# Third feed-forward stage of a Flamingo-style block stack: experts on masked inputs, accumulated in PSUM, instead of experts on all inputs, selected on VectorE

## The reference

```python
def _L2_ffn_ref(x, Wg, bg, We, be):
    ...
    probs = jax.nn.softmax(x @ Wg + bg, axis=-1)
    idx = jnp.argmax(probs, axis=-1)
    p = jnp.take_along_axis(probs, idx[..., None], axis=-1)[..., 0]
    e_idx = idx % We.shape[0]
    h = jax.nn.relu(jnp.einsum('bsd,edf->besf', x, We) + be[None, :, None, :])
    onehot = jax.nn.one_hot(e_idx, We.shape[0], dtype=x.dtype)
    out = jnp.einsum('besf,bse->bsf', h, onehot) * p[..., None]
    return out
...
    x = x + jnp.tanh(g_ffn[2]) * _L2_ffn_ref(_layernorm(x, axis=-1), L2_ffn_Wg, L2_ffn_bg, L2_ffn_We, L2_ffn_be)
```

## Time and profile before

| | |
|---|---|
| median of 3 runs | 1844.87 us |
| lowest and highest | 1843.51 and 1848.87 us |
| span of the profiled execution | 1861.1 us |
| own time of the profiled execution | not among the runs' times; its span stands 16.2 us over their median |
| mean granted clock of TensorE, whole span | 0.886 |
| stage F2, from the last addition to x of A2 to its own last one | 779.03 to 939.78 us, 160.75 us |
| PE, DVE, ACT busy, whole span | 75%, 72%, 55% |

### The profile page before, as it was taken

One profiled execution on the slowest core, in us unless ns is written; L12 is line 12 of the kernel. 1 busy time (PEld: TensorE's weight loads), 2 busy tenths in 40 slices (PEclk: granted clock), 3 DMA queues, 4 the chain that ended last, 5 costly groups with the idle time before them and its releaser, 6 DMA issues.

```text
span 1861.1 us, 35910 instructions
## 1 busy us (share of the span) xinstructions
PE 1404.8 (75%) x9844; PEld 1054.7 (57%) x9844; DVE 1333.1 (72%) x4156; ACT 1024.2 (55%) x2876; POOL 492.1 (26%) x499
## 2 busy tenths in 40 slices
PE   3677776987734446676769998989997409999995
PEld 3455554665523334433325666666666408999995
DVE  3888886888879986889945667766766455666665
ACT  3677785432425553311037777767785326777773
POOL 5433530221100001100000032232233333555451
PEclk9999998999965557978789999999999758999998
DMA  7000069300199910000000000000000052222226
GB/s 167 7 7 6 12 83 160 48 0 1 34 145 157 162 18 17 28 1 0 1 6 1 7 26 22 16 29 23 10 23 24 27 223 61 64 66 68 64 64 227
DMA packets 144711, 97.75 MB, mean 53 GB/s; under 512 B 21658, under 2 KB 133934, under 8 KB 143443
## 3 DMA queue, kind: packets, MB, share of 16 engines
q1 hardware_dynamic: 135890, 79.49, 23.2%
q0 software_dynamic: 8704, 16.87, 2.8%
HBM read 42.43 MB, written 54.93 MB: 52 GB/s over the span
## 4 chain that ended last, share of the span: by engine, by line
PE 36%; issue 31%; DVE 17%; ACT 9%; POOL 2%; DMA 1%; SPq 1%; another core or an unknown queue 1%; DVEq 1%; ACTq 0%; POOLq 0%
PE bank L1227 6%; PE bank L1219 6%; PE bank L863 5%; PE bank L912 3%; PE bank L879 3%; ACT att L1383 2%; ACT arena L1260 2%; PE bank L899 2%; PE bank L889 2%; DVE nm L1699 2%; PE bank L867 2%; DVE att L1700 1%; DVE tmp L1977 1%; DVE arena L1843 1%
## 5 line engine op out<-in xcount | busy, mean ns | idle before, releaser
L1260 ACT ACTIVATE arena<-bank 128x512 f32<-128x512 f32 (+6 forms) x440 | 255.5, 614 | 141.2 <-PE bank L1083 61.5
L540 POOL TENSOR_TENSOR rstd<-ve,mhalf 128x4 f32<-128x4 f32 x64 | 67.0, 1046 | 688.2 <-DVE ve L1680 688.2
L1383 ACT ACTIVATE att<-bank,arena 128x128 f32<-128x128 f32 x512 | 181.5, 377 | 81.8 <-DVE arena L1843 79.9
L1615 ACT ACTIVATE att<-bank,arena 128x128 f32<-128x128 f32 x576 | 164.6, 371 | 69.9 <-PE bank L1219 67.6
L639 POOL DMA_INDIRECT dispatched_rows<-arena x128 | 132.5, 1035 | 222.0 <-DVE arena L1761 153.5
L690 POOL DMA_INDIRECT expert_outputs<-arena x144 | 144.7, 1005 | 148.1 <-issue 102.9
L1260 ACT ACTIVATE xnT<-bank 128x128 f32<-128x128 f32 (+1 forms) x180 | 63.4, 352 | 190.2 <-PE bank L711 134.8
L1227 PE MATMUL bank<-arena,att 128*128 128x128 f32 x1152 | 154.1, 277 | 3.0 <-ACT att L1615 1.9
L1219 PE MATMUL bank<-xnT,arena 128*128 128x128 f32 x1152 | 154.1, 277 | 0.2 <-ACT xnT L1260 0.2
L1227 PEld LDWEIGHTS bank<-arena,att 128*128 128x128 f32 x1152 | 141.0, 193 | 5.3 <-ACT att L1615 5.3
L1219 PEld LDWEIGHTS bank<-xnT,arena 128*128 128x128 f32 x1152 | 141.6, 194 | 0.8 <-ACT xnT L1260 0.8
(11 more groups left out here) (324 smaller groups left out, 3306.1 us busy)
## 6 DMA issues: line engine op xcount, KB each, us to landing
dispatched_rows<-padf SPq DMA_DIRECT2D x16, 2128.5 KB, 35.4
arena<-dispatched_rows SPq DMA_DIRECT2D x144, 64.5 KB
cxT<-in_ctx SPq DMA_DIRECT2D x32, 256.0 KB, 2.7
arena<-in_L_ffn_w SPq DMA_DIRECT2D x8, 1024.0 KB
arena<-expert_outputs SPq DMA_DIRECT2D x8, 1024.0 KB, 13.7
expert_outputs<-arena POOLq DMA_INDIRECT x144
dispatched_rows<-arena POOLq DMA_INDIRECT x128
out_x<-x SPq DMA_DIRECT2D x8, 256.0 KB, 4.8
```

Source lines behind the costliest of these rows:

```text
L1260: copy = lambda o, i: nc.scalar.activation(o, i, ACT.Copy)
L1383: last = nc.scalar.activation(ex3_of(w, side)[:, i, :], bank[side][:, i * P:i * P + P], ACT.Exp, bias=nm3[:, w % 2, h:h + 1], accum_out=su ...
L1615: last = nc.scalar.activation(h3[:, s % 2, k * P:k * P + P], bank[s % 2][:, k * P:k * P + P], ACT.Gelu, bias=b1c3[:, s % 4, k:k + 1])
```

## The change

Each tile's normalised rows are multiplied by their one-hot column, once for each expert: eight copies of the tile, of which each row is non-zero in one alone (`xm2`). The tiles 0 and 2 of a chunk are masked by one DVE operation of 128 x 1024 each, the tiles 1 and 3 by eight ACT operations of 128 x 128 each. PE transposes the eight copies (`masked_T`, two banks), ACT copies them out of PSUM (`xmT2`), and PE multiplies each by its expert and adds all eight products, after a product of the one-hot rows with the biases, in one PSUM group (`experts`). The ReLU is ACT's (`activated`), the addition to x stays on DVE (`residual2`), one chunk late. The biases of gate and experts are split in three bf16 parts in the set-up of the stage on POOL (`parts`) and go into PSUM by small products; the exponentials take the greatest value as their bias and sum as they go. `xm2` and `xmT2` have two slots, by the tile's parity. Elsewhere the diff only lets several waits share one semaphore (`s_setup`, `F3_routing`, `F0_gate_up`), and loads bg in 3 rows and be three times.

```diff
@@ tiles @@
-        oh2 = [ar([P, CB, E2]) for _ in range(2)]
-        ohT2 = ar([E2, W])
-        acc2 = ar([P, CB, P])
+        oh2 = [ar([P, CB, 3 * E2]) for _ in range(2)]
+        ohT2 = [ar([3 * E2, W], BF16) for _ in range(2)]
+        xm2, xmT2 = ar([P, 2, E2, P]), ar([P, 2, E2, P])
+        relu2 = ar([P, CB, P])
@@ gpsimd, before the powers of F2 @@
+            def parts(whole, rest, part, mask):
+
+                for i in range(3):
+                    step(pl.tensor_copy(part[i][:, :], whole[:, :]))
+                    if i < 2:
+                        step(pl.tensor_tensor(rest[:, :], whole[:, :], part[i][:, :], ALU.subtract))
+                    whole = rest
+                for i in range(3):
+                    step(pl.tensor_scalar(part[i][:, :], part[i][:, :], mask(i), None, ALU.mult))
+                step(pl.tensor_tensor(part[0][:, :], part[0][:, :], part[1][:, :], ALU.add))
+                pl.tensor_tensor(part[0][:, :], part[0][:, :], part[2][:, :], ALU.add).then_inc(sem("F2_constants"), 1)
...
+            parts(be2, berest2, bepart2, lambda i: bemask2[:, i:i + 1])
+            parts(bg2, bgrest2, bgpart2, lambda i: ident[0:3, i:i + 1])
@@ tensor @@
+            def masked_T(c, j):
+
+                pe.wait_ge(sem("F2_masked_even" if j % 2 == 0 else "F2_masked_odd"), c * 2 + (j // 2 + 1))
+                pe.wait_ge(sem("F2_mT"), c * CB + (j + 1))
+                for e in range(E2):
+                    last = nc.tensor.transpose(bank[2 + j % 2 * 2 + e // 4][:, e % 4 * P:e % 4 * P + P], xm2[:, j % 2, e, :], ident[:, :])
+                last.then_inc(sem("F2_mT_full"), 1)
+
+            def experts(c, p, j):
+
+                pe.wait_ge(sem("F2_mT"), c * CB + (j + 3))
+                if j == 0:
+                    pe.wait_ge(sem("F2_ohT"), c + 2)
+                    pe.wait_ge(sem("F2_relu"), c + 1)
+                y = bank[6 + p][:, j * P:j * P + P]
+                nc.tensor.matmul(y, ohT2[p][:, j * P:j * P + P], bepart2[0][:, :], start=True, stop=False)
+                for e in range(E2):
+                    last = nc.tensor.matmul(y, xmT2[:, j % 2, e, :], we2[:, e * P:e * P + P], start=False, stop=(e == E2 - 1))
+                last.then_inc(sem("F2_y"), 1)
+
+            def f2(c, p, more):
+
+                for j in range(CB):
+                    if j == 0 and more:
+                        chunk_T(c + 1, 1 - p)
+                    if j == 1 and more:
+                        logits(c + 1)
+                    if j < CB - 1:
+                        masked_T(c, j + 1)
+                    experts(c, p, j)
+                if more:
+                    chosen(c + 1, 1 - p)
+                    masked_T(c + 1, 0)
@@ scalar @@
+            def exponentials(c):
+                act.wait_ge(sem("F2_onehot"), c + 1)
+                for j in range(CB):
+                    last = nc.scalar.activation(ex2[:, j, :], bank[1][:, j * P:j * P + P], ACT.Exp, bias=nmx2[:, j:j + 1], accum_out=ps2[:, j:j + 1])
+                last.then_inc(sem("F2_exp"), 1)
+
+            def masked(c, p, j):
+                act.wait_ge(sem("F2_onehot"), c + 1)
+                act.wait_ge(sem("F2_mT_full"), c * CB + (j + 1))
+                for e in range(E2):
+                    last = nc.scalar.activation(xm2[:, 1, e, :], xn2[p][:, j, :], ACT.Copy, scale=oh2[p][:, j, e:e + 1])
+                last.then_inc(sem("F2_masked_odd"), 1)
+
+            def masked_T(c, j):
+                act.wait_ge(sem("F2_mT_full"), c * CB + (j + 3))
+                act.wait_ge(sem("F2_y"), c * CB + (j + 1))
+                copy(xmT2[:, j % 2, 0:4, :], b4(2 + j % 2 * 2))
+                copy(xmT2[:, j % 2, 4:8, :], b4(3 + j % 2 * 2)).then_inc(sem("F2_mT"), 1)
...
+            def f2(c, p, more, first=False):
+                for j in range(CB):
+                    if j == 0 and not first:
+                        activated(c - 1, 1 - p)
+                    if j == 0 and more:
+                        chunk_T(c + 1)
+                    if j < CB - 1:
+                        masked_T(c, j + 1)
+                    if j == 1:
+                        masked(c, p, 3)
+                    if j == 2 and more:
+                        exponentials(c + 1)
+                if more:
+                    chosen_T(c + 1, 1 - p)
+                    masked_T(c + 1, 0)
+                    masked(c + 1, 1 - p, 1)
@@ vector @@
-                selected(c, p, 0)
-                selected(c, p, 2)
-                if next1:
-                    choose(c + 1, 1 - p, next2)
-                selected(c, p, 4)
-                selected(c, p, 6)
-                dve.wait_ge(sem("F2_bias"), c + 1)
-                step(v.tensor_tensor(acc2[:, :, :], acc2[:, :, :], b4(7), ALU.add))
-                step(v.tensor_scalar(acc2[:, :, :], acc2[:, :, :], 0.0, None, ALU.max))
...
+            def f2(c, p, more, ahead, first=False):
+                masked(c, p, 2)
+                if ahead:
+                    norm_stats(xc(c + 2))
+                    norm_var("F2")
+                if not first:
+                    residual2(c - 1, 1 - p)
+                if more:
+                    choose(c + 1, 1 - p)
+                    masked(c + 1, 1 - p, 0)
+                if ahead:
+                    normalised(c + 2, p)
+                if more:
+                    probability(c + 1, 1 - p)
```

More of the change, by code:

```diff
@@ L1153, in logits @@
                 last.then_inc(sem("F2_logits"), 1)
[L1155 to L1161, removed]
             def chosen(c, p):
                 pe.wait_ge(sem("F2_onehot"), c + 1)
+                pe.wait_ge(sem("F2_xnT"), c + 1)
@@ L1193, in _ @@
+            chunk_T(0, 0)
+            logits(0)
             chosen(0, 0)
-            experts(0, 0, range(4))
-            bias(0)
+            masked_T(0, 0)
             with pe.Fori(0, NC // 2 - 1) as i:
                 for p in range(2):
-                    f2(i * 2 + p, p, True, True)
-            f2(NC - 2, 0, True, False)
-            f2(NC - 1, 1, False, False)
+                    f2(i * 2 + p, p, True)
+            f2(NC - 2, 0, True)
+            f2(NC - 1, 1, False)
             stage_start(pe, STAGE["A3"])
@@ new lines, in _, with normalised @@
+            dve.sem_inc(sem("F2_mT_full"), 2)
+            dve.sem_inc(sem("F2_y"), 2)
+            def normalised(c, p):
+                dve.wait_ge(s_rstd, c + (1 + VAR0["F2"]))
+                if not isinstance(c, int) or c >= 2:
+                    dve.wait_ge(sem("F2_masked_odd"), c * 2 - 2)
+                for j in range(CB):
+                    last = v.tensor_scalar(xn2[p][:, j, :], xc(c)[:, j, :], mv[:, j, 0:1], rstd[:, j:j + 1], ALU.subtract, ALU.mult)
+                last.then_inc(s_xn, 1)
@@ L2247, in _ @@
                 norm_var("F2")
-                norm_apply("F2", c, xc(c), free=(sem("F2_xT"), c) if c else None)
-            choose(0, 0, False)
-            probability(0)
-            step.loop(2 * (4 + 3 + 2 * CB * 4 + 2))
-            with dve.Fori(0, NC // 2 - 1) as i:
-                step.turn(i)
+                normalised(c, c)
+            choose(0, 0)
+            masked(0, 0, 0)
+            probability(0, 0)
+            f2(0, 0, True, True, True)
+            f2(1, 1, True, True)
+            step.loop(2 * (2 + 4 + 2))
+            with dve.Fori(1, NC // 2 - 1) as i:
+                step.turn(i - 1)
                 for p in range(2):
                     f2(i * 2 + p, p, True, True)
-            step.end(NC // 2 - 1)
+            step.end(NC // 2 - 2)
             f2(NC - 2, 0, True, False)
             f2(NC - 1, 1, False, False)
+            residual2(NC - 1, 1)
             stage_start(dve, STAGE["A3"])
```

197 lines of the change are left out of this document (93 added, 104 removed).

## The result

The changed kernel takes 1873.86 us (median of 4 runs, 1872.41 to 1876.75), the kernel before 1846.87 beside it: a ratio of 1.0147, 95% interval 1.0128 to 1.0165, so 27 us slower. I had said 1851, with 1867 as the upper end: the direction was right, the size far too small, and the result is outside the range.

A forecast was written before the change was run, and what follows sets the result against it. DVE was taken to bound the stage before, a chain of PE and ACT after. At full clock 2.2 us less, plus 8 us of low clock, gave +6 on 1844.87: 1851 us, range 1840 to 1867.

The forecast's parts named there:

- the schedule: One F2 chunk at full clock: 18.0 us, 11.5 on PE and 6.5 on ACT in a chain; stage ending at 937.6.
- The other edits: Bias parts on POOL, shared semaphores and set-up DMAs: nothing, up to 2 us if POOL's operations cost half as much again.
- the sum: F2's change at full clock, -2.2 us, plus 8 us of low clock: +6 us, so 1851 us.
- the price of the bias products: Small bf16 products beside F2's logits and experts: 0.06 us each at full clock.
- the clock: PE's clock in F2: fewer falls than before, 2 us low per chunk, costing 1 us each, 8 us in all.
- rival 3: PE's clock falls in every F2 chunk, 4 to 6 us of low work each: 1859 to 1867 us; chance 0.17.
- the gap of 3.2 us: PE idle in each F2 chunk before tile 1's transposes, waiting for ACT's masks: 3.2 us.
- Rival 1: PE's clock in F2 doesn't fall despite the 3.2 us gap: 1843 to 1846 us; chance 0.20.
- rival 2: ACT's masks in F2 are cheap, each set 0.33 us less, and the clock holds: 1837 us; chance 0.10.
- rival 5: ACT's masks in F2 are dear, 0.39 us each, with some low clock: 1854 to 1862 us; chance 0.07.
- Rival 4: PE's transposes in F2 don't keep the clock up: +42 us, 1887 us; chance 0.03.

The follow-up runs named there:

- e0: The kernel before, unchanged, measured and profiled once more: ratio 0.9999 of the kernel before.
- e9: The changed kernel with its bf16 bias products filled up with zero rows to 128 rows, in the same places: 1860.95 us, 1.0080 of the kernel before.
- e5: The changed kernel without the eight bf16 bias products of each chunk, so both biases are missing in the output: 1862.19 us, 1.0079 of the kernel before.
- e4: The changed kernel plus twelve unread full fp32 products per chunk on PE before tile 1's transposes: 1867.13 us, 1.0099 of the kernel before.
- e1: The changed kernel with ACT making tile 1's masks before the copies of the one-hot rows and tile 0: 1842.47 us, 0.9977 of the kernel before.
- e11: e2 with the bf16 bias products filled up with zero rows to 128 rows: 1817.52 us, 0.9845 of the kernel before.
- e8: e2 with fp32 bias products of 1 and 8 rows in place of the bf16 ones: 1871.56 us, 1.0143 of the kernel before.
- e2: e1 with ACT also making tile 3's masks before the copies of tile 2: 1831.23 us, 0.9921 of the kernel before.

## Why the prediction was wrong

**What held.** DVE bound before and doesn't after. After the change the chunk is a chain of PE and ACT, with the gaps where the schedule had them. Eight masks on ScalarE take 2.44 us (2.43 forecast), a mask on DVE 1.22 (1.2). PE's transposes of masked tiles wait behind ACT's masks, 36.3 us in 16 times. No table load stands in F2. The other edits cost nothing (e0). DVE's and ACT's shares were forecast badly, 60% and 65%, against 73.03 / 191.67 = 38% and 50%; the sum didn't rest on them.

**What failed: the price of the bias products.** "A bf16 product of 128 columns 0.06 (eight in 0.62)" took a row of products with 128 rows, one behind the other, for one of 24 or 3 rows between full ones. I looked at the type and the columns and not at the rows. I had also named the danger with a bound too low ("at the 0.22 of a full one +1.3 us a chunk"): a dearer price than a full product's wasn't in my thoughts. At full clock the chunk takes 20.24 us in place of 18.0; with 128 rows (e9) it takes 18.65, and without the bias products (e5) 17.77. So eight of them cost 2.47 us a chunk, 0.31 each, where the sum had 0.5 for all eight; the few rows keep the weight loads from overlapping, a wait that the sum didn't have.

**What was mis-sized: the clock.** The forecast had 2 us of low clock a chunk, 8 us in the stage. A fall came in nearly every chunk, as in rival 3, which priced it at 16 to 24 us; it cost a little less than that. The mechanism was named, the number of falls was guessed too low. Six chunk periods run from 800.47 to 933.08 (starts of L1179): 22.1 us on average, 1.9 over the full-clock chunk.

**The account.** The schedule had F2 at 158.6 us at full clock (779.03 to 937.6); it took 191.7. Of the 33.1:

- The start, 1.4: tile 1's transposes begin 20.0 us into the stage (804.25 less 784.23), not 18.6. Without the bias products (e5) they begin 18.3 us in (802.91 less 784.64), so this is theirs too.
- Longer chunks at full clock, 16.9: seven of 2.24, and four products of 0.3 in the last. By e5 the bias products have 1.99 of each 2.24 (2.47 less the 0.48 that the sum had); 0.25 a chunk lies in my other prices.
- Clock, 14.8, the rest. The same from the last chunk's transposes of tile 1 (958.40, after 3.57 us of waiting): they begin 154.15 us after the first chunk's; less seven times 20.24 that is 12.5, and the chunk behind them takes 17.5 us (to 975.90) in place of 14.0, 1.2 of it for the bias. Part of it lies in the first chunk, where the clock stayed low until 810.3. And e4's trace gave 14.8 back.

```profile
958.40 1.97 PE L1203 MATMUL bank<-ident,arena 128*128 128x128 f32 x8 [3.57 <-ACT arena L1632]
```

So of the 25 us by which the stage came out later than forecast, some 16.5 are the bias products, start included, 7 the clock and under 2 the other prices. With the gap of 3.2 us gone (e1), every chunk from 828.3 us on has full clock: the falls went with it.

The rivals. Rival 1 (the clock holds) and rival 2 (cheap masks) fell with the rows of L1632 and the clock; rival 5 (dear masks) with the 2.44 us. Rival 4 isn't borne out: in e11 the chunk is at full clock though forty transposes, at 0.11 us some 4 of its 13.7 us, stand in it. By the rule of the Trainium skill that stood behind this rival ("TensorE: Matmul & The Clock Gate", "Part 4: PE-mode transpose") they wouldn't count for the clock; no run here shows that they don't.

## What to carry to other kernels

When work moves to another engine, write the new chain down, and look on each engine for work that needs nothing of the step before it and stands behind it all the same: one line moved on ScalarE was worth 37 us of the stage and 31 of the whole time, more than the whole loss. Take the price of an instruction from a row with the same shape in all three sizes, rows, columns and type, and the same neighbours; fill small products up to 128 rows or put them together before they go between full ones. And count a gap on TensorE like this one of 3.2 us twice, once for itself and once for what runs at half clock behind it; the gaps of 1.4 us that e1 kept left the clock at 1.00.

## What the runs showed of the hardware that I had not expected

- A product of few rows between products of 128 rows costs its neighbour too: 0.41 us each at full clock in fp32 (0.22 with 128 rows), 0.57 a pair with bf16 (0.34 with 128 rows). Four few-row products together took 0.32 us. Where the row count changes (changed kernel), the next weight load starts with its own product; where it stays (e9), 0.06 to 0.11 us ahead of it.
- Rows of zeros cost less than a changing row count: e9 does more multiplications than the changed kernel, and its chunk at full clock is 1.59 us shorter.
- fp32 products of 1 and 8 rows between full ones bring the granted clock down with no gap between PE's records (e8: from full to half in the middle of the logits, 0.80 in F2; e2 with bf16 products of few rows, 0.92). Whether the rows or the time lost between the products does it stays open; no run parts the two.
- Products that nobody reads can make a stage faster: 96 of them, F2 14.8 us less, by the clock, and the whole time 6.7 less.
